# Moving one product of a seven-product period three value products later in a fused sparse-attention layer

## The reference

```
h   = max(layernorm(x), 0)
lQ, lK, lV = masked_x @ Wlq, h @ Wlk, h @ Wlv + blv
s   = where(adj, lQ @ lK.T / 16, -1e9)
m   = max(rowmax(s), global, es)
res = exp(s - m) / denom @ lV + ge/denom * gV + ee/denom * eV
out = x + max(res, masked_x)
```

## Time and profile before

| | us |
|---|---|
| median of 3 runs | 731.57 (731.06 to 731.91) |
| the profiled execution, its own time | 731.89 |
| its span, first to last instruction | 730.0 |
| PE busy in the span | 722.1 (99%) |
| DVE busy | 564.5 (77%) |
| ACT busy | 532.3 (73%) |
| POOL busy | 433.6 (59%) |
| mean granted TensorE clock | 0.999 of full speed |

### The profile page before, as it was taken

How to read it: one execution, slowest core, us unless ns; L and a number is a source line. 1 busy time by engine, 2 the same in 40 slices (tenths; PEclk the granted TensorE clock), 3 DMA queues, 4 the chain that set the end, 5 groups by cost and what they waited for, 6 DMA issues and landing times.

```text
span 730.0 us, 15027 instructions
## 1 busy us (share of the span) xinstructions
PE 722.1 (99%) x5248; PEld 511.8 (70%) x5248; DVE 564.5 (77%) x1347; ACT 532.3 (73%) x709; POOL 433.6 (59%) x300
## 2 busy tenths in 40 slices
PE   8999999999999999999999999999999999999998
PEld 7667566667766777776767677776776767676777
DVE  6975988777887788878878787878878887977643
ACT  6885967858677776776788677777777677677690
POOL 4779889455465455555555564556545555654493
PEclk9999999999999999999999999999999999999999
DMA  9782877869779888968878798989888798878697
GB/s 299 135 178 76 162 154 148 160 139 214 158 159 176 168 162 152 202 146 189 154 175 165 159 190 142 203 150 180 175 171 159 158 198 146 184 160 188 115 170 166
DMA packets 364716, 121.93 MB, mean 167 GB/s; under 512 B 324832, under 2 KB 364640, under 8 KB 364640
## 3 DMA queue, kind: packets, MB, share of 16 engines
q1 hardware_dynamic: 364096, 120.44, 81.7%
q10 hardware_dynamic: 544, 0.52, 0.2%
HBM read 36.57 MB, written 4.19 MB: 56 GB/s over the span
## 4 chain that ended last, share of the span: by engine, by line
PE 81%; issue 5%; DVE 5%; POOL 4%; ACT 3%; DMA 2%; DVEq 0%; SPq 0%; ACTq 0%; POOLq 0%
PE ps_u L1124 13%; PE ps_u L1128 13%; PE ps_u L1126 13%; PE ps_x L1022 6%; PE ps_x L1023 6%; PE ps_x L1021 6%; PE ps_q L945 4%; PE ps_v L1021 3%; PE ps_v L1023 3%; PE ps_v L1022 3%; POOL p_base L619 2%; PE ps_w L1021 2%; PE ps_w L1022 2%; PE ps_w L1023 2%; DVE st L1339 1%
## 5 line engine op out<-in xcount | busy, mean ns | idle before, releaser
L619 POOL TENSOR_TENSOR p_base<-s,p_base 128x1024 f16<-128x1024 f32 x112 | 242.4, 2164 | 229.4 <-ACT p_base L822 220.4
L1124 PE MATMUL ps_u<-v_rows,pT_base 128*128 128x256 f16 x968 | 263.8, 273 | 0.7 <-DMA pT_base<-bias 0.7
L1128 PE MATMUL ps_u<-v_rows,pT_base 128*128 128x256 f16 x968 | 263.8, 273 | 0.0
L1126 PE MATMUL ps_u<-v_rows,pT_base 128*128 128x256 f16 x968 | 263.8, 273 | 0.0
L785 ACT ACTIVATE bias<-adj,big 128x1024 f32<-128x1024 uint8 x127 | 156.5, 1237 | 130.5 <-DVE bmax L1492 128.5
L798 ACT ACTIVATE s<-s,negm,invc 128x1024 f32<-128x1024 f32 x128 | 157.0, 1227 | 8.9 <-DVE negm L1548 8.9
L822 ACT ACTIVATE p_base<-s 128x1024 f16<-128x1024 f32 x122 | 129.0, 1057 | 6.2 <-DMA hW<-p_base 1.3
L1124 PEld LDWEIGHTS ps_u<-v_rows,pT_base 128*128 128x128 f16 x968 | 94.7, 98 | 53.2 <-DMA pT_base<-bias 0.9
L1126 PEld LDWEIGHTS ps_u<-v_rows,pT_base 128*128 128x128 f16 x968 | 94.7, 98 | 52.2
L1492 DVE CUSTOM_DVE_ANT_0 s<-ps_x,bias 128x512 f32<-128x512 f32 x128 | 87.1, 685 | 48.1 <-PE ps_x L1023 44.6
L1128 PEld LDWEIGHTS ps_u<-v_rows,pT_base 128*128 128x128 f16 x968 | 94.7, 98 | 11.0
(11 more groups left out here) (242 smaller groups left out, 1262.4 us busy)
## 6 DMA issues: line engine op xcount, KB each, us to landing
adj<-adj SPq DMA_DIRECT2D x64, 256.0 KB, 3.2
pT_base<-p_base SPq DMA_TRANSPOSE x238, 3.2
s<-x SPq DMA_DIRECT2D x7, 512.0 KB, 7.8
f32q<-mx SPq DMA_DIRECT2D x14, 256.0 KB, 3.7
xm<-x SPq DMA_DIRECT2D x14, 256.0 KB, 3.1
xm<-mx SPq DMA_DIRECT2D x14, 256.0 KB, 3.5
out<-t_sb SPq DMA_DIRECT2D x14, 256.0 KB, 2.5
mxT_f<-mxT SPq DMA_DIRECT2D x4, 256.0 KB, 3.2
```

The lines of the kernel that those rows point to most:

```text
L619: nc.gpsimd.tensor_tensor(p_rows(u)[:, 1], s32[:, p % NS, u % 2], p_rows(u)[:, 0], ALU.subtract).then_inc(s_plo, 1)
L1124: nc.tensor.matmul(acc, turn[:, 0, j], v_rows[:, kc, 0:D], start=opens, stop=False, skip_group_check=True)
L1126: nc.tensor.matmul(acc, turn[:, 0, j], v_rows[:, kc, D:2 * D], start=False, stop=False, skip_group_check=True)
L1128: done = nc.tensor.matmul(acc, turn[:, 1, j], v_rows[:, kc, 0:D], start=False, stop=end, skip_group_check=True)
```

## The change

`p5(p)` moves from between value products 3 and 4 to directly ahead of `p6(p)`, behind value product 6: three value products later. `p7(p-1)` moves from between value products 1 and 2 to between 2 and 3: one value product later. `p1`, `p6`, `p4`, `p2` and `p3` keep their place among the value products, except in period 12, where two key sums stand between value products 5 and 6, and `p5` moves past them too. No instruction is added or removed, all other engines keep their orders, and no wait changes: each product takes its own wait along.

```
-                    p_times_v(p, 0, 2)
+                    p_times_v(p, 0, 3)
                     if wino(old):
                         p7(old)
-                    p_times_v(p, 2, 4)
-                    if p < NPER:
-                        p5(p)
-                    p_times_v(p, 4, 6)
+                    p_times_v(p, 3, 6)
                     if p == PC:
                         keys_t3_sum(2)
                         keys_t3_sum(3)
...
                     p_times_v(p, 6, 7)
                     if p < NPER:
+                        p5(p)
                         p6(p)
```

## The result

The changed kernel takes 737.43 us (median of 6 runs, 734.92 to 737.89) against 731.65 us before (6 runs, 731.06 to 731.91): ratio 1.0072, 95% interval 1.0061 to 1.0083. It is slower by 5.8 us. The profiled execution took 737.49 us, its span is 735.6 us where it was 730.0.

What follows compares the result with a forecast made beforehand. PE, busy 99% of the span, was taken as the bound. 731.57 - 0.98 (period 19's `p5` wait) + 2.0 (losses from DVE operations held by POOL) = 732.6 us, range 730.5 to 737.6.

Steps and rivals of the forecast that it cites:

- the catch in step 1: DVE's `cq` or `cqs` held by POOL's second `p_low`, making `out12` late: 0.1 to 0.35 us a row pair, chance 0.48.
- no difference that can be told: Sign of the whole change: time within 1.46 us of the kernel before, chance 0.52.
- the first rival: In step 2 both `side_rows` operations are held, `out21` is late, `p1` of step 3 waits: 735.6 to 737.6 us, chance 0.36.
- the gain of 0.98: Period 19: `p5` loses 1.09 us waiting for its bank; moved later, only 0.11 us of the wait is left.
- PE's work: On PE: the same 5248 matmuls, two fewer boundaries between products and value products each period, at 0 each.
- the new starts: On DVE, with `p5` 0.98 us later: `add22` starts 4.43 after `p1` instead of 3.45, side work 5.04 instead of 4.06.
- The walk round the steps: Steps 0 to 3, which DVE side operations POOL holds: middle 0.2 us a row pair in ten row pairs, 2.0 us.
- the double catch: Step 2: POOL's first `p_low` holds one `side_rows` operation, `q_low` the second, so `out21` starts at o + 9.35.
- The rule for the loss: `p1` after step 2 loses o + 0.3 us, o being `out12`'s entry to step 2, between -0.3 and 0.6.
- caught in its turn: Step 3: `mx_scale`, late because its rows load behind a later `q_low`, is held by POOL: another 0.2 us.

Runs made afterwards that it cites:

- experiments 1: Against the kernel before, one product moved alone: `p5` three value products later 737.04 us, ratio 1.0073; `p7` one later 731.24 us, ratio 0.9998.
- experiment 3: Changed kernel with the first two `side_rows` operations of step 2 ahead of `add22` on DVE instead of behind it: 732.09 us, ratio 1.0007.
- experiment 2: Kernel before with `p5` two value products later, 733.84 us, ratio 1.0029, or one later, 732.78 us, ratio 1.0021; `p7` unmoved.

## Why the prediction came out as it did

The time lies in the range (730.5 to 737.6), at its upper end, but the stated likeliest, 732.6, was 4.8 us too low; most chance stood on small losses from the catch in step 1 (0.48) and, of the signs, on no difference that can be told (0.52), and neither came. What happened is the first rival, "the wait moves to `p1`", chance 0.36, at 735.6 to 737.6. That its sum fits so closely is in part luck: with the losses measured it would be 731.57 - 0.98 + 5.49 = 736.1, and the time is above this mainly because the gain of 0.98 didn't come.

**PE's work, `p7`, the new starts.** Right: no boundary or product costs anything by itself (experiments 1 and 3), `p7` alone is at 0.9998, and `add22` starts 4.43 after `p1` in most periods.

**The gain of 0.98 us in period 19.** Wrong. The step that failed is "it should: what stands ahead of it, `out11(18)`, waits for POOL and not for PE". POOL itself follows the `out12` of the period before, over ACT. In the changed kernel that one starts at 209.78, 2.84 after its `p1` instead of 1.88, and everything behind it moves along (DVE, periods 18 and 19, against the earlier trace rows):

```profile
209.78 0.68 DVE L1490 CUSTOM_DVE_ANT_0 s<-ps_v,bias 128x512 f32<-128x512 f32 x1
...
216.50 0.69 DVE L1490 CUSTOM_DVE_ANT_0 s<-ps_w,bias 128x512 f32<-128x512 f32 x1 [1.79 <-POOL p_base L619]
...
220.65 0.68 DVE L1490 CUSTOM_DVE_ANT_0 s<-ps_v,bias 128x512 f32<-128x512 f32 x1
```

From `out12` to `out12` it is 10.87 here and 10.88 before: the loop keeps its length, the lateness goes through it undiminished, and `p5` waits as long as before.

**The catch in step 1.** Right where its starting point held. Period 21, DVE, then POOL, against the earlier trace rows:

```profile
246.18 0.16 DVE L1401 TENSOR_TENSOR rtrue<-rmax,mu 128x2 f32<-128x2 f32 x1
...
246.78 2.06 DVE L1412 TENSOR_TENSOR cqs<-cq,mu 128x2 f32<-128x2 f32 x1
...
249.44 0.67 DVE L1490 CUSTOM_DVE_ANT_0 s<-ps_x,bias 128x512 f32<-128x512 f32 x1
```

```profile
246.70 2.13 POOL L619 TENSOR_TENSOR p_base<-s,p_base 128x1024 f16<-128x1024 f32 x1 [0.55 <-ACT p_base L822]
```

`rtrue` passes, `cqs` is caught, `out21` starts at 249.44, 9.01 after `p1` (9.0 worked out), `p1(22)` goes just in time; `out12` enters step 2 at 1.87 (1.9) and step 3 at 2.97 (3.0), and `p5` loses 0.12 (0.16).

**The walk round the steps.** Here is the step that made the size wrong: I took this row pair as the pattern of all ten. It isn't a pattern. A table of where `out12` starts after the period's `p1`, worked out from the starts in the two traces, and of what the next `p1` or this `p5` lost ("before" is periods 28 to 31 of the kernel before):

```
             step 0   step 1   step 2   step 3   lost
before        -0.45    -0.96    -0.05    1.6      0
periods 20-23 -0.45    -0.84     1.87    2.97     0.12 (p5, step 3)
periods 24-27 -0.12    -0.42     0.60    1.44     0.96 (p1, step 3)
periods 28-31  0.51     0.00     0.75    2.58     0
periods 32-35 -0.38    -0.68     0.35    1.44     0.71 (p1, step 3)
periods 36-39  0.51     0.00     0.74    2.58     0
```

Step 3 of period 23, entered late, gives back -0.12 and not -0.45. So step 1 is entered at -0.42, its first `p_low` ends 0.7 us later than in period 21 (6.42 after `p1` against 5.72), catches `rtrue` for 0.68 us and lets the rest of `q_rows` through, as the rival has it ("or is caught by the first one again"); step 2 is entered at 0.60, and there the double catch waits. From period 24 to 51 row pairs with and without it take turns, 84.2 us apart in the timeline (386.99, 471.19, 555.39 are the caught `p1`). Only periods 21 and 53 of the ten in step 1 had the catch by the second `p_low` that I had given to all. The rule for the loss held: o + 0.3 gives 0.90, 0.65 for entries at 0.60 and 0.35, measured 0.96 and 0.71; entries at 0.74 lost nothing.

**Two places without a row in the prediction.** The last row pair has `side_rows` in period 62 but no `q_rows` in period 61 and no `q_low` in 62; the second `p_low` catches instead, 0.84 us at period 63. And `mx_scale`, "caught in its turn", was put at 0.2 us a row pair; in period 51 two of its operations were caught one after the other, for 1.71 and 1.99 us, and `p1(52)` lost 0.59. DVE, then POOL:

```profile
560.98 0.69 DVE L1464 TENSOR_REDUCE mmax<-f32q 128x2 f32<-128x512 f32 x1 [0.45 <-DMA f32q<-mx]
561.70 1.71 DVE L1466 TENSOR_SCALAR mcl<-mmax 128x2 f32<-128x2 f32 x1
...
563.72 1.99 DVE L1475 TENSOR_TENSOR mu<-mpow,unw 128x4 f32<-128x4 f32 x1
```

```profile
561.25 2.13 POOL L619 TENSOR_TENSOR p_base<-s,p_base 128x1024 f16<-128x1024 f32 x1 [5.14 <-ACT p_base L822]
563.56 2.13 POOL L619 TENSOR_TENSOR p_base<-s,p_base 128x1024 f16<-128x1024 f32 x1 [0.18 <-ACT p_base L822]
```

**Two readings that were too wide.** The prediction lets all of DVE's side operations on SBUF stand still while POOL works. `mmax`, a reduction of 512 columns from SBUF, is not held: in the kernel of experiment 3 it starts at 557.87, inside a `p_low` of 557.60 that lasts 2.13 us, and takes 0.69; so it does wherever it starts inside a `p_low`, ten times in all traces (0.68 to 0.69). `mcl`, which also has one SBUF tensor as input, is held there, 1.17 us against 0.17 free. And "0.03 us between the end of `q_rows` and POOL's next start" is not its end: the last operation, `rpow`, starts at 329.55 in the trace before, 0.02 ahead of the `p_low` of 329.57, and lasts 0.16.

**The page.** The Trainium skill, "GPSIMD Engine Reference", section "Key points", names contention of GpSimd with VectorE operations that have two SBUF inputs or run in a two-port mode. The traces agree (0.48 us free, 2.40 and 1.99 caught, 0.67 to 0.69 always for the `add` and `out` operations, which read PSUM) and show the form it takes here: a full hold to about the end of POOL's operation. The section cited says nothing of the form; another page of the Trainium skill does, "SBUF — State Buffer", section "SBUF: two separate sides": whichever of the two engines starts first has the shared pair of SBUF ports for its whole instruction. That is what experiment 2 shows: DVE 0.01 us behind is held for 2.39, DVE 0.10 us ahead takes 0.48 and POOL's operation 2.37 instead of 2.13.

Left open: whether the spread of the changed kernel's runs (734.92 to 737.89, 2.97 us against 0.85 before) comes from the number of row pairs caught, or from a late load ahead of `mx_scale`. The profile of `p5` alone, of a run at 736.22, has five `p1` waits and none at `p1(52)`, where the changed kernel's, at 737.49, has seven, which fits; it wasn't tested.

## What to carry to other kernels

An instruction that is covered in its own period can still decide which later instruction is held, so follow a delay round the whole loop of engines (here DVE to ACT to POOL to DVE) until it comes back to its starting point, and use what it comes back as, not the old value. Before DVE work on SBUF is shifted, compare its new start with the starts of GpSimd's operations: 0.1 us ahead it took 0.48 us, 0.01 us behind it took 2.4. Where an engine has to wait for a later product anyway, put its side work ahead of that wait.

## What was not expected of the hardware

In the kernel with `q_low` last, PE stood for 3.1 us from 313.2 on. The columns are PE, weight loads, DVE, ACT, POOL busy, then the granted clock, DMA share and GB/s:

```profile
313.00:316.30 3.30, 0.40 (x4) 0.10 (x2) 2.57 (x9) 1.72 (x3) 0.53 (x1) 1.00 0.88 203
316.30:320.20 3.90, 3.85 (x15) 2.15 (x16) 3.29 (x9) 3.01 (x4) 2.72 (x2) 0.56 1.11 222
320.20:324.00 3.80, 3.80 (x29) 2.55 (x27) 2.24 (x4) 3.74 (x7) 1.29 (x1) 1.00 0.83 184
```

After the pause the granted clock was 0.56 of full speed in the mean for 3.9 us, near the lower of its two levels (1.2 of 2.4 GHz). Value matmuls went 0.21 us apart instead of 0.11, and 1.7 us more were lost (`p5(28)` starts 5.26 after `p1`, not 3.58). The shorter waits of this study (up to 1.65 us) show no such slow stretch behind them.
